# Half 1's causal convolution as four TensorE products in a fused state-space, expert and attention kernel

## The chip, the cores and the metric

The kernel runs on one core of one Trainium2 chip. The metric is the device time of one execution in microseconds; every time in this text is in microseconds unless marked otherwise. PE is TensorE, DVE is VectorE, ACT is ScalarE, POOL is GpSimd and SP is SyncE.

## The reference, cut to what matters

Four stages follow each other, each added to `x` of shape (4, 256, 256): a selective state-space layer gated by the layer norm of `x`, a routed network with 32 experts (8 per token), cross attention with 16 heads, and a network with 16 experts (2 per token) and a shared one. Only the first stage is touched:

```python
x = einsum('ed,bld->bel', in_proj_w, ctx)            # 256 channels
xc = causal depthwise convolution of x, 4 taps        # per channel
u = silu(xc + conv_b)
x_dbl = einsum('ke,bel->bkl', x_proj_w, u)            # 8 rows dt, 16 B, 16 C
delta = softplus(dt_proj_w @ x_dbl[:8] + dt_proj_b)
# per channel and state n: state = state*exp(delta*A[n]) + delta*u*B[n];  y += state*C[n]
y = (y + D*u) * silu(layernorm(x))
```

## The kernel before, in words

**Tiling.** The 1024 tokens are two halves of 512 (two batches of 256 each). Channels stand on the 128 partitions, in two blocks (c = 0, 1), so one array of a half is 128x512 per block. The scan over time is one VectorE instruction (`tensor_tensor_scan`, L1544) per half and state over both blocks, 128x1024; there are 16 states (`DS`), and thus 16 steps per half. A step `n` consists of: ScalarE's decay exp(delta*A) (`scan_decay`, L1085, into one of two pairs of PSUM banks for half 0), the row of B spread over the partitions by a DMA (`b_rows`), GpSimd's product of it with delta*u (`scan_drive`, L2183; VectorE makes the first itself, L1534), the scan (L1544), the read-out with the row of C (`scan_read`, L1554) and TensorE's turning sum of the read-outs (`y_sum`, L571). Decay n+2 waits for scan n, drive n+1 for read-out n-1, and row n+3 of B for the drive that frees its buffer.

**Ahead of the first scan.** For each half and block TensorE makes `in_proj @ ctx` (`project_in`, L534), ScalarE the last tap (`first_tap`, L1053), VectorE three further taps in place, each over both batches (`convolve`, L1470), ScalarE the silu (`activate_u`, L1058). Then x_dbl (`project_x_dbl`, L542) is copied by ScalarE (`move_x_dbl`, L1049), dt is one product on a bias product (`bias_dt` L559, `project_dt` L551), ScalarE takes exp and ln (`activate_delta`, L1069 and L1071), VectorE bounds it (L1517) and multiplies with u (L1523). `x_dbl`'s rows go to DRAM by `store_bc` and come back as `b_rows` and `c_rows`. Both halves are prepared before or just within the first steps of the first scan; the normalisation of `x` for the gate (statistics L1479, L1484, L1486 on VectorE, the power -1/2 on GpSimd, `scale_norm`, L2141, shift L1510) lies in the same stretch.

**What sets the order.** Every engine has its own instruction stream, executed in the order written; semaphores join them. In the first scan ScalarE's stream holds, after the decay of step n+2, work for the gate (`normalise_z`, `activate_z`), TensorE's the folding of the attention weights (`fold_turn`, `fold_multiply`, at the steps listed in `folds_at`: from step 4, two at steps 7, 10 and 13), and SyncE's the loads: at every step one row of B, one row of C, and, at their steps, weights of the first expert layer (`fetch(0)` to `fetch(3)`, 384 KB each), raw attention weights (`load_fold`, 384 + 256 KB) and folded ones (`store_fold`, 512 KB). A row of B or C is 256 KB. ScalarE swaps its function table (`preload_act_table_set`) between silu, log/exp and exp.

After the first scan VectorE gates y, adds it to `x` and makes the next statistics; the turned `x` gives the router its logits, and the second half's scan runs between the first expert products. From about 200 us on TensorE works nearly without a gap to the end.

## Time and profile before

| | us |
|---|---|
| median of 3 runs (lowest to highest) | 672.03 (671.31 to 673.62) |
| span of the profiled execution | 671.5 |
| PE busy in it (share of the span) | 619.0 (92%) |
| DVE busy | 485.6 (72%) |
| ACT busy | 412.6 (61%) |
| POOL busy | 305.0 (45%) |

The profile shows one execution by its span, from the first to the last instruction; the page gives no other time of its own for it. An engine's busy share is a mean over stages with different limits. So the profile is to be read by stage: which engine has no idle time there, and what ended the wait of the one that had.

### The profile page before, as it was taken

Reading aid. Unit: us, or ns where it says so; the run is one execution under the profiler, and the core shown is the slowest. Engines: PE = TensorE matmul, PEld = TensorE weight load, DVE = VectorE, ACT = ScalarE, POOL = GpSimd, SP = SyncE. Lnnn points to the kernel's source line nnn. Section 1 sums busy time; section 2 is a strip of 40 time slices with the busy share of each in tenths; the row PEclk is TensorE's granted clock in tenths of the full one; section 3 lists DMA queues with packets and bytes.
Section 4 is the critical chain, followed back from the end, with each engine's and each line's share of the span. In section 5 each row is a group of like instructions: output and inputs, shape, how many; then the busy total and the mean of one; then the engine's idle time right before and its main releaser. Section 6 shows DMA issues by size and latency. Waiting matters only on the chain.

```text
span 671.5 us, 11179 instructions
## 1 busy us (share of the span) xinstructions
PE 619.0 (92%) x3740; PEld 517.2 (77%) x3740; DVE 485.6 (72%) x1048; ACT 412.6 (61%) x846; POOL 305.0 (45%) x304
## 2 busy tenths in 40 slices
PE   6768669999999999999999999999999998899994
PEld 2356445566777788888888999999989988789983
DVE  5999889999987665546457766767759774785464
ACT  4976565855535645445457787777867768654441
POOL 1456630022254434445436656665545788540214
PEclk9668988999999999999999999999999999999998
DMA  6686744666764364454319533224101112255654
GB/s 199 189 291 226 280 162 132 198 202 205 211 171 137 97 175 136 136 156 155 125 48 313 189 120 117 79 79 138 53 32 33 56 64 87 80 173 156 197 160 132
DMA packets 58135, 98.90 MB, mean 147 GB/s; under 512 B 7000, under 2 KB 26976, under 8 KB 58080
## 3 DMA queue, kind: packets, MB, share of 16 engines
q1 hardware_dynamic: 56544, 94.00, 44.1%
q0 software_dynamic: 1536, 4.20, 1.9%
q8 instruction: 31, 0.51, 0.3%
q14 instruction: 24, 0.20, 0.1%
HBM read 78.51 MB, written 19.66 MB: 146 GB/s over the span
## 4 chain that ended last, share of the span: by engine, by line
PE 65%; DVE 19%; issue 5%; ACT 4%; POOL 3%; DMA 2%; DVEq 0%; POOLq 0%; SPq 0%; ACTq 0%
PE bank L101 18%; PE bank L102 17%; PE bank L103 17%; DVE state L1544 7%; PE bank L886 3%; PE bank L974 3%; DVE read_out L1554 3%; PE bank L938 2%; PE bank L571 1%; DVE u_sb L1470 1%; PE bank L680 1%; DMA b_rows<-bc_scratch 1%; ACT probs L1341 1%; DVE stats L1479 1%; DVE head_out_lo L1461 1%
## 5 line engine op out<-in xcount | busy, mean ns | idle before, releaser
L2149 POOL TENSOR_TENSOR w_lo<-w_raw,w_hi 128x512 fp32r<-128x512 f32 (+1 forms) x78 | 120.6, 1549 | 160.5 <-ACT w_hi L1049 80.0
L101 PE MATMUL bank<-xt_hi,w_hi 128*128 128x512 f32 x256 | 104.7, 409 | 1.6 <-POOL w_lo L2149 1.0
L103 PE MATMUL bank<-xt_hi,w_lo 128*128 128x512 f32 x256 | 101.1, 395 | 0.0
L102 PE MATMUL bank<-xt_lo,w_hi 128*128 128x512 f32 x256 | 100.9, 394 | 0.0
L1049 ACT ACTIVATE w_hi<-w_raw 128x512 fp32r<-128x512 f32 (+1 forms) x78 | 56.6, 726 | 45.9 <-PE bank L103 45.0
L1341 ACT ACTIVATE probs<-scores,row_min 128x256 f32<-128x256 f32 x128 | 63.8, 501 | 17.4 <-DVE row_min L1963 17.4
L2260 POOL TENSOR_TENSOR probs<-probs,row_scale 128x512 f32<-128x512 f32 x64 | 66.6, 1040 | 5.0
L1963 DVE CUSTOM_DVE_ANT_0 scores<-bank,mask_bias 128x256 f32<-128x256 f32 x128 | 48.8, 420 | 17.3 <-PE bank L103 17.3
L571 PEld LDWEIGHTS bank<-identity,read_out 128*128 128x128 f32 x272 | 36.3, 159 | 30.4 <-DVE read_out L1554 18.6
L1049 ACT ACTIVATE probs_t_hi<-bank 128x512 fp32r<-128x512 f32 x64 | 38.2, 597 | 32.6 <-PE bank L886 32.3
L101 PEld LDWEIGHTS bank<-xt_hi,w_hi 128*128 128x128 f32 x256 | 48.2, 188 | 12.4 <-POOL w_lo L2149 3.6
L103 PEld LDWEIGHTS bank<-xt_hi,w_lo 128*128 128x128 f32 x256 | 48.1, 188 | 11.7
L571 PE MATMUL bank<-identity,read_out 128*128 128x128 f32 x272 | 41.6, 306 | 15.8 <-DVE read_out L1554 13.2
L102 PEld LDWEIGHTS bank<-xt_lo,w_hi 128*128 128x128 f32 x256 | 48.3, 189 | 8.5 <-issue 0.2
L1461 DVE TENSOR_TENSOR probs_t_lo<-bank,probs_t_hi 128x512 fp32r<-128x512 f32 x64 | 44.1, 689 | 10.4 <-ACT probs_t_hi L1049 10.2
L2183 POOL TENSOR_TENSOR drive<-delta_u,b_rows 128x1024 f32<-128x1024 f32 x16 | 38.4, 2401 | 28.4 <-DVE read_out L1554 17.5
L2257 POOL TENSOR_TENSOR row_scale<-row_scale,any_valid 128x2 f32<-128x2 f32 x64 | 12.5, 195 | 76.3 <-DVE row_scale L1955 76.1
L1461 DVE TENSOR_TENSOR hidden_lo<-bank,hidden_hi 128x512 fp32r<-128x512 f32 x34 | 23.4, 690 | 31.4 <-ACT hidden_hi L1049 31.4
L101 PE MATMUL bank<-probs_t_hi,ctx_tok_hi 128*128 128x256 f32 x128 | 41.4, 323 | 4.7 <-DVE head_out_lo L1461 4.6
L1554 DVE TENSOR_TENSOR read_out<-state,c_rows 128x1024 f32<-128x1024 f32 x32 | 42.5, 1330 | 0.6
L1842 DVE TENSOR_TENSOR bank<-gated,bank 128x512 f32<-128x512 f32 x34 | 23.6, 695 | 26.0 <-PE bank L103 22.6
L1207 ACT ACTIVATE gated<-bank 128x512 f32<-128x512 f32 x48 | 28.7, 597 | 22.2 <-PE bank L103 22.1
(259 smaller groups left out, 1834.2 us busy)
## 6 DMA issues: line engine op xcount, KB each, us to landing
w_raw<-in_ffn_w SPq DMA_DIRECT2D x46, 384.0 KB, 3.5
b_rows<-bc_scratch SPq DMA_DIRECT2D x32, 256.0 KB, 4.9
c_rows<-bc_scratch SPq DMA_DIRECT2D x32, 256.0 KB, 4.3
w_raw<-fold_scratch SPq DMA_DIRECT2D x32, 256.0 KB, 2.7
experts<-in_ffn_w SPq DMA_DIRECT2D x16, 384.0 KB, 4.3
route_bc<-route_scratch SPq DMA_DIRECT2D x31, 192.0 KB, 3.4
...
```

Source lines behind the costliest of these rows:

```text
L101: e.matmul(out, w_hi, m_hi, start=first, stop=False)
L102: e.matmul(out, w_hi, m_lo, start=False, stop=False)
L103: return e.matmul(out, w_lo, m_hi, start=False, stop=last)
L571: last = e.matmul(ps[:, l * DI + c * P:l * DI + (c + 1) * P], tile[:, c, t:t + P], identity[:, :], is_transpose=True, start=n < 0 and l + ...
L1049: e.activation(out, source, ACT.Copy).then_inc(sem(name), 1)
L1341: last = e.activation(probs[i % 3][:, r, :], scores_sb[i % 2][:, r, :], ACT.Exp, scale=-1.0, bias=row_min[i % 2][:, r:r + 1], accum_out=ro ...
L1461: e.tensor_tensor(out_lo, source, out_hi.bitcast(F32), ALU.subtract).then_inc(sem(name), 1)
L1544: e.tensor_tensor_scan(flat2(state[i % 2][:, :, :]), flat2(factor[:, :, :]), flat2(drive[i % 2][:, :, :]), 0.0, ALU.mult, ALU.add).then_in ...
L1554: e.tensor_tensor(read_out[n % 4][:, :, :], state[i % 2][:, :, :], c_rows[i % 3][:, :].unsqueeze(1).broadcast_to([P, EH, HT]), ALU.mult).t ...
L1963: e.tensor_tensor_reduce(scores_sb[i % 2][:, r, :], bank[4 + i % 2][:, r * SEQ:(r + 1) * SEQ], mask_bias[:, half * HB + b, :], -SCALE, 3.0 ...
L2149: e.tensor_tensor(lo[:, 0:n], w_raw[(p - WHOLE) % RAW][:, 0:n], hi[:, 0:n].bitcast(F32), ALU.subtract).then_inc(sem("w_lo"), 1)
L2260: e.tensor_tensor(probs[i % 3][:, :, :], probs[i % 3][:, :, :], row_scale[i % 3][:, :].unsqueeze(2).broadcast_to([P, 2, SEQ]), ALU.mult).t ...
```

## The change

- Half 0 goes first on all engines. `ctx`'s half 0 is loaded from ScalarE's queue, the small weights come second and the projections third on SyncE, half 1's `ctx` and the raw attention weights later.
- Half 0's block 0 is projected, tapped and convolved batch by batch; the order of waits between the six small taps leaves one other tap between two that depend on each other. VectorE instead of ScalarE copies its x_dbl.
- Half 1 is no longer projected and convolved in two steps. TensorE turns the taps (`turn_conv`), VectorE copies them (`conv_rows`), TensorE spreads each tap's row over the partitions (`spread_conv`, with a selection matrix made on GpSimd), VectorE multiplies `in_proj` by it (`scale_in_proj`, one 128x1024 instruction) and TensorE sums four products of 512 columns per block, each with `ctx` shifted by one token more (`convolve`). The silu reads that bank.
- Half 1's u is made at step 0 of the first scan, its x_dbl is moved at step 1, its delta comes at steps 3 to 5 (before the read-outs of 4 and 5), `activate_z` at step 5 instead of 2.
- GpSimd makes delta*u of half 0's block 0. Half 1's variance and half 0's shift lie between scan 0 and read-out 0, half 1's shift after it.
- Folding starts at step 5, with two at 7, 9, 11 and 13; `fetch(0)` and `fetch(1)` move to steps 4 and 5, `fetch(2)` and `fetch(3)` behind the first scan.

The diff, cut to its core:

```diff
@@ -492,8 +498,10 @@
...
-        FOLD_FROM, FOLD_STEPS = 4, 2 * KV_HEADS
-        FOLD_TWICE = (7, 10, 13)
+        FOLD_FROM, FOLD_STEPS = 5, 2 * KV_HEADS
+        FOLD_TWICE = (7, 9, 11, 13)
+        LATE_U, LATE_DELTA, Z_AT = 0, 3, 5
...
@@ -504,8 +512,12 @@
...
         def dt_bank(h, c):
-            return ((7, 0), (6, 1))[h][c]
+            return ((7, 0), (7, 6))[h][c]
...
@@ -527,29 +539,57 @@
...
+            def turn_conv():
+
+                at.wait_ge("consts", 3)
+                at.wait_ge("ld_small", 16)
+                for c in range(EH):
+                    last = e.transpose(bank[4][0:DC, c * P:(c + 1) * P], small_sb[:, c, 0:DC], identity[:, :])
+                last.then_inc(sem("conv_in"), CONV_TURNED)
+
+            def spread_conv(taps):
+
+                at.wait_ge("conv_in", CONV_ROWS)
+                at.wait_ge("gpsimd_chain", 3)
+                for j in taps:
+                    e.matmul(bank[4 + j // 2][:, j % 2 * DI:(j % 2 + 1) * DI], conv_pick[:, j * P:(j + 1) * P],
+                             conv_rows[:, :], start=True, stop=True).then_inc(sem("conv_in"), 1)
+
+            def convolve(c):
+
+                at.wait_ge("conv_in", CONV_SCALED)
+                at.wait_ge("ld_ctx1", 16)
+                ps = take(6 + c, ("u", EH + c + 1))
+                out_of = ps.rearrange("p (b s) -> p b s", b=HB)
+                ctx_of = ctx_sb[:, HT:].rearrange("p (b s) -> p b s", b=HB)
+                for back in range(DC):
+                    last = e.matmul(out_of[:, :, back:], conv_in[:, DC - 1 - back, c * P:(c + 1) * P],
+                                    ctx_of[:, :, :SEQ - back], start=back == 0, stop=back == DC - 1)
+                last.then_inc(sem("conv_in"), 1)
...
+            def project_x_dbl(h, c):
...
-                ps = take(6, ("x_dbl_sb", h + 1))
-                for c in range(EH):
-                    at.wait_ge("u", 2 * h + c + 1)
-                    last = e.matmul(ps[0:DR + 2 * DS, :], x_proj_sb[:, c, :], u_sb[:, h, c, :],
-                                    start=c == 0, stop=c == EH - 1)
-                last.then_inc(sem("x_dbl"), 1)
-
-            def project_dt(h):
+                ps = take(6, ("x_dbl_sb", h + 1)) if c == 0 else bank[6]
+                at.wait_ge("u", 2 * h + c + 1)
+                last = e.matmul(ps[0:DR + 2 * DS, :], x_proj_sb[:, c, :], u_sb[:, h, c, :],
+                                start=c == 0, stop=c == EH - 1)
+                if c == EH - 1:
+                    last.then_inc(sem("x_dbl"), 1)
...
@@ -781,25 +821,33 @@
...
-            for c in range(EH):
-                project_in(0, c)
-            for c in range(EH):
-                project_in(1, c)
...
-            at.wait_ge("consts", 3)
+            turn_conv()
+            for b in range(HB):
+                project_in(0, b, slice(b * SEQ, (b + 1) * SEQ))
+            project_in(1, 0, slice(0, HT))
+            spread_conv(range(2))
+            project_x_dbl(0, 0)
+            spread_conv(range(2, DC))
+            bias_dt(0, 0)
+            project_x_dbl(0, 1)
+            bias_dt(0, 1)
             for c in range(EH):
-                bias_dt(0, c)
-            project_x_dbl(0)
-            project_dt(0)
-            project_x_dbl(1)
+                project_dt(0, c)
             for c in range(EH):
-                bias_dt(1, c)
-            project_dt(1)
+                convolve(c)
             for n in range(-1, DS):
                 y_sum(0, n)
-                if n == 1:
+                if n == LATE_U:
+                    for c in range(EH):
+                        project_x_dbl(1, c)
+                if n == LATE_DELTA - 1:
+                    for c in range(EH):
+                        bias_dt(1, c)
+                        project_dt(1, c)
+                if n == Z_AT - 1:
                     turn_z(0)
                     turn_z(1)
...
@@ -1048,15 +1096,19 @@
...
-            def first_tap(h, c):
-                at.wait_ge("proj_in", 2 * h + c + 1)
...
+            def first_tap(c, b, tokens, nth):
+                at.wait_ge("proj_in", nth)
+                e.activation(u_sb[:, 0, c, tokens], bank[in_bank(c, b)][:, tokens], ACT.Copy,
                              scale=conv_w[DC - 1][:, c:c + 1]).then_inc(sem("first_tap"), 1)
...
-                at.wait_ge("conv", 2 * h + c + 1)
-                e.activation(u_sb[:, h, c, :], u_sb[:, h, c, :], ACT.Silu,
-                             bias=conv_b[:, c:c + 1]).then_inc(sem("u"), 1)
+                if h == 0:
+                    at.wait_ge("conv", HB + c)
+                    source = u_sb[:, 0, c, :]
+                else:
+                    at.wait_ge("conv_in", CONV_SCALED + c + 1)
+                    source = bank[6 + c][:, :]
+                e.activation(u_sb[:, h, c, :], source, ACT.Silu, bias=conv_b[:, c:c + 1]).then_inc(sem("u"), 1)
...
@@ -1226,35 +1277,40 @@
...
+            e.dma_start(ctx_sb[:, 0:HT], ctx_t[:, 0:HT]).then_inc(sem("ld_ctx0"), 16)
             e.preload_act_table_set("silu_and_others")
...
-            first_tap(0, 0)
-            first_tap(0, 1)
-            first_tap(1, 0)
+            for b in range(HB):
+                first_tap(0, b, slice(b * SEQ, (b + 1) * SEQ), b + 1)
+            first_tap(1, 0, slice(0, HT), HB + 1)
             activate_u(0, 0)
-            first_tap(1, 1)
             activate_u(0, 1)
-            move_x_dbl(0)
-            activate_u(1, 0)
-            activate_u(1, 1)
             e.preload_act_table_set("natural_log_exp_and_others")
             e.activation(decay[:, :, :], a_log, ACT.Exp).then_inc(sem("a_exp"), 1)
             activate_delta(0)
-            move_x_dbl(1)
             for n in range(2):
                 scan_decay(0, n)
-            activate_delta(1)
             make_skip(0)
-            normalise_z(0)
             for n in range(DS):
                 if n + 2 < DS:
                     scan_decay(0, n + 2)
-                if n == 0:
+                if n == LATE_U:
+                    e.preload_act_table_set("silu_and_others")
+                    activate_u(1, 0)
+                    activate_u(1, 1)
+                    e.preload_act_table_set("natural_log_exp_and_others")
+                if n == LATE_U + 1:
+                    normalise_z(0)
+                    move_x_dbl(1)
+                if n == LATE_U + 2:
                     normalise_z(1)
-                if n == 2:
+                if n == LATE_DELTA:
+                    activate_delta(1)
+                if n == Z_AT:
+                    e.preload_act_table_set("silu_and_others")
                     activate_z()
                     e.preload_act_table_set("exp_and_others")
...
@@ -1460,20 +1516,43 @@
...
+            def convolve(c, back, batches):
...
+                late = u_sb[:, 0, c, :].rearrange("p (b s) -> p b s", b=HB)[:, batches, back:]
+                x_in = bank[in_bank(c, batches.start)][:, :].rearrange("p (b s) -> p b s", b=HB)[:, batches, :SEQ - back]
+                return e.scalar_tensor_tensor(out=late, in0=x_in, scalar=conv_w[DC - 1 - back][:, c:c + 1], in1=late,
+                                              op0=ALU.mult, op1=ALU.add)
...
+            def convolve_by_batch():
+
                 for back in range(1, DC):
...
+                    for b in range(HB):
+                        at.wait_ge("first_tap", b + 1)
+                        if back > 1:
+                            at.wait_ge("vector_chain", own.count - (HB - 1 if back < DC - 1 else HB - 1 - b))
+                        last = convolve(0, back, slice(b, b + 1))
+                        if back < DC - 1:
+                            own.step(last)
+                        else:
+                            last.then_inc(sem("conv"), 1)
+
+            def convolve_whole():
+
+                at.wait_ge("first_tap", HB + 1)
+                for back in range(1, DC):
+                    own.settle()
+                    last = convolve(1, back, slice(0, HB))
                     if back < DC - 1:
                         own.step(last)
-                        own.settle()
                 last.then_inc(sem("conv"), 1)
...
+            def scale_in_proj():
+
+                at.wait_ge("conv_in", CONV_SPREAD)
+                at.wait_ge("ld_in_proj", 16)
+                e.tensor_tensor(conv_in[:, :, :], banks[:, 4:6, :].rearrange("p k (j d) -> p (k j) d", j=2),
+                                in_proj_sb[:, :].unsqueeze(1).broadcast_to([P, DC, DI]),
+                                ALU.mult).then_inc(sem("conv_in"), 1)
...
@@ -1855,32 +1934,44 @@
...
-            for c in range(EH):
-                convolve(0, c)
-            for c in range(EH):
-                convolve(1, c)
+            at.wait_ge("conv_in", CONV_TURNED)
+            e.tensor_copy(conv_rows[:, :], bank[4][0:DC, 0:DI]).then_inc(sem("conv_in"), 1)
+            at.wait_ge("ld_small", 16)
+            convolve_by_batch()
+            convolve_whole()
             at.wait_ge("ld_x0", 16)
             for j in range(HC):
                 chunk_stats(0, j)
             find_variance(0)
-            at.wait_ge("conv", 2 * HALVES)
+            at.wait_ge("x_dbl", 1)
+            e.tensor_copy(x_dbl[:, 0:HT], bank[6][0:DR + 2 * DS, :]).then_inc(sem("x_dbl_sb"), 1)
+            scale_in_proj()
+            at.wait_ge("a_exp", 1)
+            e.tensor_scalar(decay[:, :, :], decay[:, :, :], -1.0, None, ALU.mult).then_inc(sem("decay_ready"), 1)
+            at.wait_ge("conv", HB + 1)
+            at.wait_ge("conv_in", CONV_SCALED)
             e.memset(banks[:, 2:6, :].rearrange("p k (b s) -> p (k b) s", b=HB)[:, :, 0:1],
                      0.0).then_inc(sem("decay_ready"), 1)
             at.wait_ge("ld_x1", 16)
-            for j in range(HC):
+            for j in range(2):
                 chunk_stats(1, j)
-            find_variance(1)
-            at.wait_ge("a_exp", 1)
-            e.tensor_scalar(decay[:, :, :], decay[:, :, :], -1.0, None, ALU.mult).then_inc(sem("decay_ready"), 1)
-            find_z_shift(0)
-            make_delta_u(0)
+            make_delta(0, 0)
+            chunk_stats(1, 2)
+            make_delta(0, 1)
+            make_delta_u(0, 1)
             scan_drive(0, 0)
-            find_z_shift(1)
+            chunk_stats(1, 3)
             for n in range(DS):
                 scan_state(0, n)
+                if n == 0:
+                    find_variance(1)
+                    find_z_shift(0)
+                if n in (LATE_DELTA + 1, LATE_DELTA + 2):
+                    make_delta(1, n - LATE_DELTA - 1)
+                    make_delta_u(1, n - LATE_DELTA - 1)
                 scan_read(0, n)
                 if n == 0:
-                    make_delta_u(1)
+                    find_z_shift(1)
...
@@ -2156,6 +2247,13 @@
...
+            own.step(e.memset(conv_pick[:, :], 1.0))
...
@@ -2189,8 +2287,13 @@
...
             split_gates()
             scale_norm(0, 1)
+            at.wait_ge("delta", 1)
+            at.wait_ge("u", 1)
+            e.tensor_tensor(delta_u[:, 0, 0, :], delta[:, 0, 0, :], u_sb[:, 0, 0, :],
+                            ALU.mult).then_inc(sem("delta_u"), 1)
+            scan_drive(0, 1)
             scale_norm(1, 2)
-            for n in range(1, DS):
+            for n in range(2, DS):
                 scan_drive(0, n)
             scan_drive(1, 0)
...
@@ -2373,38 +2476,39 @@
                 e.dma_start(out_dram[:, t:t + 2, :], x_tok[:, t:t + 2, :]).then_inc(sem("out_stored"), 16)
 
             load(in_proj_sb[:, :], in_proj_t, "ld_in_proj")
-            for h in range(HALVES):
-                load(ctx_sb[:, h * HT:(h + 1) * HT], ctx_t[:, h * HT:(h + 1) * HT], f"ld_ctx{h}")
             load(small_sb[:, :, :], ssm_small, "ld_small")
+            load(x_proj_sb[:, :, :], x_proj_t, "ld_proj")
+            load(dt_proj_sb[:, :], dt_proj_t, "ld_proj")
             for c in range(EH):
                 e.dma_start(dt_row[0:1, c * P:(c + 1) * P], ssm_small[:, c, DC + 2:DC + 3].rearrange("p a -> a p"),
                             allow_slow_non_contiguous=True).then_inc(sem("ld_proj"), 16)
             for h in range(HALVES):
                 load(x_tok[:, h * HC:(h + 1) * HC, :], x_dram[:, h * HC:(h + 1) * HC, :], f"ld_x{h}")
-            load(x_proj_sb[:, :, :], x_proj_t, "ld_proj")
-            load(dt_proj_sb[:, :], dt_proj_t, "ld_proj")
+                if h == 0:
+                    load(ctx_sb[:, HT:], ctx_t[:, HT:], "ld_ctx1")
             load(gate_raw[:, :, :], gate_t, "ld_late")
             load(cent_raw[:, :, :], centroids_t, "ld_late")
             load(bias_bc[:, :], rows(gate_bias, P), "ld_late")
             load(mask_u8[:, :, :].rearrange("p b s -> p (b s)"), rows(key_mask, P), "ld_late")
-            for g in range(2):
-                load_fold(g)
 
 
             store_bc(0)
             for n in range(3):
                 load_b(0, n)
                 load_c(0, n)
+                if n < 2:
+                    load_fold(n)
             load_b(0, 3)
-            store_bc(1)
             for n in range(DS):
                 if n > 0:
                     load_b(*divmod(n + 3, DS))
                 load_c(*divmod(n + 3, DS))
-                if n < SPLIT:
-                    fetch(n)
+                if n == LATE_U + 2:
+                    store_bc(1)
                 if n + 2 < FOLD_RAW:
                     load_fold(n + 2)
+                if 0 <= n - FOLD_RAW + 1 < 2:
+                    fetch(n - FOLD_RAW + 1)
                 for g in range(KV_HEADS):
                     if g >= FOLD_RAW and fold_step[2 * (g - FOLD_RAW) + 1] + 1 == n:
...
@@ -2413,6 +2517,8 @@
...
             load_c(1, 3)
+            for p in range(2, WHOLE):
+                fetch(p)
             store_fold(KV_HEADS - 2)
             load_b(1, 5)
             load_c(1, 4)
```

## Rows read from the trace of the kernel before

**Rows 1.** The page's chain that ended last, share of the span by engine and line

```profile
PE 65%; DVE 19%; issue 5%; ACT 4%; POOL 3%; DMA 2%; DVEq 0%; POOLq 0%; SPq 0%; ACTq 0%
```

**Rows 2.** Instructions in order of time, VectorE (start, duration, line, shapes, count, idle before)

```profile
7.38 8.96 DVE L1470 SCALAR_TENSOR_TENSOR u_sb<-bank,small_sb,u_sb 128x510 f32<-128x510 f32 x12 [7.38 <-ACT u_sb L1053]
...
24.22 2.29 DVE L1544 TENSOR_TENSOR_SCAN state<-bank,drive 128x1024 f32<-128x1024 f32 x1
...
27.69 1.28 DVE L1517 SCALAR_TENSOR_TENSOR delta<-delta,bank 128x512 f32<-128x512 f32 x2
28.88 2.58 DVE L1523 TENSOR_TENSOR delta_u<-delta,u_sb 128x512 f32<-128x512 f32 x2
...
87.86 1.37 DVE L1554 TENSOR_TENSOR read_out<-state,c_rows 128x1024 f32<-128x1024 f32 x1
```

**Rows 3.** Groups by line, VectorE, 24.2 to 89.2 us

```profile
L1544 DVE TENSOR_TENSOR_SCAN state<-bank,drive 128x1024 f32<-128x1024 f32 x16 | 36.5, 2279 | 2.3 <-POOL drive L2183 2.3
```

**Rows 4.** Order of time, SyncE's queue, before the first scan

```profile
2.17 0.43 SPq L2300 DMA_DIRECT2D small_sb<-in_ssm_small  x1
...
17.06 0.33 SPq L2300 DMA_DIRECT2D b_rows<-bc_scratch  x1
```

**Rows 5.** Order of time, TensorE, before the first scan

```profile
4.42 6.61 PE L534 MATMUL bank<-ctx_sb,in_proj_sb 128*128 128x512 f32 x8 [4.42 <-DMA ctx_sb<-in_ctx_t]
...
12.87 1.91 PE L542 MATMUL bank<-u_sb,x_proj_sb 128*40 128x512 f32 x4
15.46 2.13 PE L551 MATMUL bank<-x_dbl,dt_proj_sb 8*128 8x512 f32 x4 [0.68 <-ACT x_dbl L1049]
17.52 3.41 PE L542 MATMUL bank<-u_sb,x_proj_sb 128*40 128x512 f32 x4
```

**Rows 6.** Order of time, ScalarE, before the first scan and at its third step

```profile
11.94 0.72 ACT L1058 ACTIVATE u_sb<-u_sb,small_sb 128x512 f32<-128x512 f32 x1 [0.15 <-DVE u_sb L1470]
...
17.12 1.28 ACT L1243 ACT_TABLE_LOAD   x1
...
18.55 0.58 ACT L1069 ACTIVATE delta<-bank 128x512 f32<-128x512 f32 x1
...
37.15 1.30 ACT L1085 ACTIVATE bank<-delta,decay 128x510 f32<-128x510 f32 x2 [1.80 <-DVE state L1544]
```

**Rows 7.** One line's instructions, ns min/median/max; last row b_rows' landing in us

```profile
L1554 DVE TENSOR_TENSOR read_out<-state,c_rows x16: 1225/1371/2636, 26.5 to 87.9; 128x1024 f32<-128x1024 f32 x16
...
L1523 DVE TENSOR_TENSOR delta_u<-delta,u_sb x4: 679/685/1973, 21.6 to 30.8; 128x512 f32<-128x512 f32 x4
...
DMA to landing us min/median/max: 3.2/5.6/7.8
```

**Rows 8.** Order of time, GpSimd, at three places

```profile
18.35 1.05 POOL L2141 TENSOR_TENSOR rstd<-rstd,half_power 128x4 f32<-128x4 f32 x1 [5.03 <-DVE rstd L1486]
...
24.25 2.34 POOL L2183 TENSOR_TENSOR drive<-delta_u,b_rows 128x1024 f32<-128x1024 f32 x1 [2.96 <-DVE drive L1534]
...
95.92 2.92 POOL L2141 TENSOR_TENSOR rstd<-rstd,half_power 128x4 f32<-128x4 f32 x1 [7.77 <-DVE rstd L1486]
```

**Rows 9.** Windows: busy time of each engine, granted clock, DMA share, GB/s

```profile
15.00:20.00 5.00, 4.54 (x7) 1.25 (x8) 4.86 (x20) 4.58 (x8) 1.05 (x1) 0.72 0.38 81
...
25.00:30.00 5.00, 2.43 (x7) 0.94 (x6) 4.97 (x5) 4.49 (x9) 3.66 (x2) 0.50 0.49 98
```

**Rows 10.** Who waited for whom, 14 to 90 us: total, times, longest

```profile
POOL drive L2183 <- DMA b_rows<-bc_scratch: 7.9, 3, 3.7
```

**Rows 11.** Chain that ended last, 60 to 80 us (start, us, what)

```profile
67.94 7.22 DMA b_rows<-bc_scratch
...
75.28 3.10 POOL drive L2183
...
78.46 2.30 DVE state L1544
```

**Rows 12.** DMA of the stretch 16 to 50 us, all queues

```profile
DMA packets 3954, 8.11 MB, mean 238 GB/s; under 512 B 458, under 2 KB 458, under 8 KB 3951
```

65 lines of the change are left out of this document (33 added, 32 removed).

## The prediction, made before the changed kernel ran

> **What bounds the kernel now.** I read the page first: the chain that ended last is 65% TensorE and 19% VectorE [rows 1]. TensorE's share is nearly all the 128x512 split products that come after the state-space layer; the change touches none of them. So the change can only help by letting that part begin earlier, and the question is how much earlier the first scan (half 0, 16 states) ends. The trace in order of time answers what sets that: VectorE is busy, with one gap of 2.3, from its first convolution tap at 7.38 us to the last read-out of the first scan, which ends at 87.86 + 1.37 = 89.23 us [rows 2]. Within the scan (24.22 to 89.23) it does 16 scans of 2.28 [rows 3] and 16 read-outs of 1.23 to 1.37; one pair takes 3.5 to 3.6. Behind the scan stands one unbroken chain (gate, add, statistics, turn, router, second scan, then TensorE), so I count each microsecond at 89.23 as one microsecond at the end. The profiled span is 671.5; it lies 0.5 under the median of the runs, 672.03, and I carry that 0.5 over. A difference under 0.3% (2.0 us) can't be told from no change.
>
> **Half 0 until its first scan.** ctx half 0 is now issued by ScalarE's queue, about when SyncE issues in_proj, and the small weights go second on SyncE instead of fourth (2.17 us [rows 4]); three issues of about 0.45 sit before it now, one afterwards, so it lands about 0.9 sooner. TensorE's first product began at 4.42 and eight instructions took 6.61 [rows 5], 1.7 per 512 columns at first. Now two small transposes of the taps come first (0.5, my estimate from these products' speed), then the two batches of channel block 0 as 256-column products, 0.85 each. First outputs at about 5.7, 6.5 and, for block 1, 8.2 us.
> Convolution on VectorE: 12 instructions took 8.96 [rows 2], 0.75 each. Kept for half 0 are 6 halves (0.75 less 256 elements at the 512 elements' rate, 0.48) and 3 whole ones: 2.9 + 2.3 = 5.2, but with gaps for the late first taps. Laid end to end behind first taps of 0.7 the last ends at 11.8, and the second silu near 12.5, against 11.94 + 0.72 = 12.66 before [rows 6]. **Splitting by batch alone gains almost nothing.**
> TensorE now has two tap spreads and a bias product between the two x_dbl products; they delay the second by about 0.5, so x_dbl is there at 14.0, against 12.87 + 1.91 = 14.78 [rows 5]. VectorE copies it now (not in the trace as such; between ScalarE's 0.58 for a 512-column read of a bank [rows 6] and a tap's 0.75, I take 0.65), dt of block 0 is there at 15.9, against 15.46 and half of 2.13 before [rows 5].
> The real gain is on ScalarE: before, its exp of dt began at 18.55, because half 1's taps and silus and the table load at 17.12 stood ahead [rows 6], two microseconds after dt was there. Now the table is loaded at about 13.8, exp begins at 16.0, and four activations of 0.6 end at 18.4, against 20.9. VectorE has free time for the scaling of in_proj (1024 elements a row, as one read-out of 1.23 [rows 7]: it ends at 15.9), the decay sign, and most of half 1's statistics. Then: second delta 19.15, delta_u 19.9 (block 0's goes to GpSimd, about half of a drive's 2.34 [rows 8], beside it), first drive 21.2, last statistic, first scan at 21.6. The b_rows load: its store issues at 14.8, it at 16.5 instead of 17.06 [rows 4], and 3.2 later (the fastest landing [rows 7]) it is in at 19.7, in time. **Start of the scan: 24.22 - 21.6 = 2.6 gained.** Bounds: 0.7 if only x_dbl's own lead (14.78 - 14.0) gets through; 4.5 if all of the six removed convolution instructions (6 x 0.75) do. I keep 2.6.
>
> **Half 1 inside the scan.** The eight tap products (4 taps x 2 blocks, each one 512-column fp32 product) follow dt from 16.9. Between 15 and 20 the granted clock was 0.72, from 25 to 30 it was 0.50, the lower of the two levels (1.2 GHz) [rows 9]; the same four x_dbl instructions took 1.91 and then 3.41 [rows 5]. So a product costs 0.86 at full clock and 1.7 at half: the eight take 6.9 to 13.7 and end at 23.8 to 30.6. I take 25.6 (half clock until about 20.8, then full, since these are full-array products back to back). ScalarE wants them at 26.5: decay of state 2 after the first scan, then a table load (1.28). Its extra work per step is 3.96 (two loads, two silus), 2.7, 2.1, 2.4 and 5.0 (z), against 2.2 free a step (3.52 less 1.30 for the decay [rows 6]) and 3.45 of one-time lead; the backlog peaks near 2.9, so it is hidden at no cost. If the lead were used up each further microsecond would be on the path.
> Delta of half 1: the four VectorE instructions cost 1.28 + 2.58 before [rows 2], where one delta_u ran beside a drive on GpSimd and took 1.97 instead of 0.69 [rows 7]. Moved between scan and read-out, when GpSimd is done, they cost 2.7, and I add 0.6 for the first log being late (bias and dt now come after step 2's turns at half clock): 0.3 to 0.5 gained at most. I take 0.3.
> **A new knot at step 0.** half 1's variance and half 0's shift are now between scan 0 and read-out 0: 0.7. And shift 1 after read-out 0 waits for GpSimd's power, which is behind drive 1 on GpSimd. A power took 1.05 alone but 2.92 beside a VectorE scan with both inputs in SBUF [rows 8]; a read-out ran 2.64 instead of 1.37 beside a late drive [rows 7]. I reckon drive 1 at 23.0 to 25.35 (its row is queued behind c_rows 0 and a fold load), the read-out held until 25.35 and ending 26.5, the power ending 27.4, shift, scan 1 at 27.6. Without any of this scan 1 would begin at 25.2. Cost 2.4; ends 0.7 (only the moved instructions) and 3.5 (another 1.1, a read-out, lost).
> The Trainium skill, SBUF — State Buffer, "Who interferes with whom", says that a VectorE instruction with two SBUF inputs and a GpSimd one that reads SBUF take turns, the first holding the port for its whole length. This trace agrees (2.64, 2.92). By a mere sharing of bandwidth the knot would be 0.7 and the time 1.7 less, 666.9.
>
> **Loads.** Three drives waited for b_rows, 7.9 in all [rows 10]; the first two, at steps 5 and 6, stretched two read-outs by 0.45 and (to 2.64 [rows 7]) 1.4. Steps 0 to 3 carried a whole weight piece (384 KB) each beside three folds (640 KB). Now those steps hold only folds, and two of the pieces come at steps 4 and 5, two after the scan. So the 1.85 is gained; ends 0 and 1.85. The later stall: b_rows for state 13 took 7.22 from issue to landing behind a fold store and fold load, its drive began at 75.28, scan 13 at 78.46 [rows 11], VectorE idle for 2.3 [rows 3]. The new plan spreads the doubled folds over 7, 9, 11, 13: from row 10 to row 12, 2816 KB must land in 10.9 us, before 4992 KB in 18.0; both about 0.27 MB/us, near the rate that failed. So a stall stays, a step earlier. I take 1.3 of it, so 1.0 gained; ends -2.3 and +2.3. The two whole pieces issued after the scan are first used some 15 us later, and landings took 5 to 8: covered. If that cover were gone, gate 2 would be late by the difference.
>
> **Sum.** -2.6 (start) -0.3 (delta) +2.4 (knot) -1.85 (early rows) -1.0 (late row) = **-3.35**. Span 671.5 - 3.35 = 668.1; with the 0.5, 668.6.
>
> **Rivals.**
> (a) *More.* The knot shrinks to 0.7 (row 1 lands in time and the power slips in during the scan) and no row is late: -2.6 -0.3 +0.7 -1.85 -2.3 = -6.4: 665.7, and up to 664 with the start at its better end. For: the early DMA load is lighter by 1.3 MB. Against: the power's 2.92 [rows 8] and the 7.22 of one row [rows 11]. Chance 0.17.
> (b) *The change does not do what it says / is given back.* Half 1's products stay at half clock to 30.6; x_dbl and dt of half 1 then take 3.4 each, the first log comes 1.4 later, and the start gains only 0.7 because x_dbl of half 0 is what sets it: -3.35 + 1.4 + 1.9 = -0.05, 672.0; with either alone -1.5 to -1.95, so 670.1 to 670.5. For: clock 0.50 in this stretch before [rows 9]. Against: TensorE now works where it was idle. Chance 0.17. The Trainium skill, TensorE: Matmul & The Clock Gate, "What's actually happening", says that the default is the throttled state and that activity releases it; by that rule these products release it themselves, and the forecast stands; this trace has both levels, but no stretch of such products here.
> (c) *Slower.* Late b_rows decide: the first rows are now interleaved with two fold loads (issued around 18 us, before they went at 8 us under the convolutions), and folds follow in steps 0, 1, 2. If the queue gives less than one fold and two rows (1152 KB) in 3.6 us, which is 0.32 MB/us, each of drives 1 to 6 is late, and a late one costs up to 2.3 idle plus 1.3 for the blocked read-out. From 16 to 50 us the mean was 238 GB/s [rows 12]. One such drive (3.6) beyond what I took evens the gain out; two at 2.7 each make it 668.6 + 5.4 = 674.0. For: loads of b_rows took 5.6 us to land at the median [rows 7]. Against: these rows are each issued over 4 us before use. Chance 0.09.
> The forecast itself keeps 0.57.
>
> **Numbers.** Predicted 668.6. The forecast's own ends are 667 and 670; the range reaches to (a)'s and (b)'s cases: 664.8 to 671.4. Faster by over 0.3% (under 670.0): 0.52 of the forecast, (a) whole, a little of (b): 0.72. Within 0.3%: 0.20. Slower: 0.08.
>
> **What would show it.** The first scan of half 0 starts near 21.6, the second near 27.6 after a gap, the last read-out ends near 85.8; the eight tap products lie between 16.9 and 25.6; ScalarE loads a table four times in the scan's first 30 us; no VectorE idle before the scans of steps 3 to 9. Wrong would be: scans waiting for the decay on ScalarE (the lead was used up), a first scan still after 23, or several scans that wait for a GpSimd drive.

## The result, and the profile after

The changed kernel takes **679.12** (median of 4 runs, 677.90 to 680.78) against 672.03: ratio **1.0105** [1.009, 1.0121], slower by 7.1. Forecast were 668.6 and a range from 664.8 to 671.4. It was run again on two other chips: 1.0113 [1.009, 1.0135] (678.95 against 671.67) and 1.0111 [1.0092, 1.013] (687.58 against 679.12). So 1.011 is the yardstick for all that follows. Ratios to the kernel before on the same chip are compared, since on three of the five chips that were used the kernel before itself takes 7 to 8.5 longer. A ratio is estimated from all runs and can differ by up to 0.002 from the quotient of the two medians given beside it (here 687.58/679.12 is 1.0125); no smaller difference between two ratios is relied on.

The page's chain of the profiled execution (span 676.2, its time 678.25) is that of before [rows 1] but for a larger share of TensorE and a smaller one of VectorE:

```profile
PE 67%; DVE 16%; issue 5%; ACT 4%; POOL 3%; DMA 3%; SPq 0%; DVEq 0%; POOLq 0%; ACTq 0%
```

VectorE in order of time (start, duration, engine, line and operation, idle before it and what ended it), which answers to [rows 2]:

```profile
15.94 0.68 DVE L1947 COPY x_dbl<-bank 40x512 f32<-40x512 f32 x1 [2.24 <-PE bank L582]
...
20.93 0.69 DVE L1595 SCALAR_TENSOR_TENSOR delta<-delta,bank 128x512 f32<-128x512 f32 x1 [2.29 <-ACT delta L1123]
...
22.64 0.69 DVE L1595 SCALAR_TENSOR_TENSOR delta<-delta,bank 128x512 f32<-128x512 f32 x1 [0.68 <-ACT delta L1123]
...
25.57 2.27 DVE L1623 TENSOR_TENSOR_SCAN state<-bank,drive 128x1024 f32<-128x1024 f32 x1
27.76 0.36 DVE L1563 BATCH_NORM_AGGREGATE mean_var<-stats 128x2 f32<-128x6 f32 x4
28.15 0.83 DVE L1565 TENSOR_SCALAR rstd<-mean_var 128x4 f32<-128x4 f32 x1
28.90 0.15 DVE L1589 SCALAR_TENSOR_TENSOR z_shift<-mean_var,rstd 128x4 f32<-128x4 f32 x1
28.97 1.21 DVE L1633 TENSOR_TENSOR read_out<-state,c_rows 128x1024 f32<-128x1024 f32 x1
31.09 2.31 DVE L1589 SCALAR_TENSOR_TENSOR z_shift<-mean_var,rstd 128x4 f32<-128x4 f32 x1 [0.91 <-POOL rstd L2232]
33.33 2.28 DVE L1623 TENSOR_TENSOR_SCAN state<-bank,drive 128x1024 f32<-128x1024 f32 x1
...
47.53 0.69 DVE L1595 SCALAR_TENSOR_TENSOR delta<-delta,bank 128x512 f32<-128x512 f32 x1 [1.25 <-ACT delta L1123]
...
91.56 1.37 DVE L1633 TENSOR_TENSOR read_out<-state,c_rows 128x1024 f32<-128x1024 f32 x1
...
95.67 1.30 DVE L1642 TENSOR_TENSOR bank<-bank,z_gate 128x512 f32<-128x512 f32 x2 [1.61 <-PE bank L611]
...
103.37 1.38 DVE L1575 TENSOR_SCALAR x_norm<-x_tok,mean_var,rstd 128x256 f32<-128x256 f32 x4 [0.83 <-POOL rstd L2232]
```

Three things stand in it. Before, VectorE had no wait from its first tap to the first scan; now it waits 5.2 in three places for half 0's own x_dbl and dt. The two four-element instructions at 28.15 and 31.09, 0.17 and 0.15 when alone, take 0.83 and 2.31. And the gate waits 1.61 for TensorE, twice the 0.8 of before. GpSimd shows what the small ones stood beside, a drive each time:

```profile
26.60 2.36 POOL L2281 TENSOR_TENSOR drive<-delta_u,b_rows 128x1024 f32<-128x1024 f32 x1 [3.63 <-DMA b_rows<-bc_scratch]
29.06 1.99 POOL L2232 TENSOR_TENSOR rstd<-rstd,half_power 128x4 f32<-128x4 f32 x1
31.03 2.35 POOL L2281 TENSOR_TENSOR drive<-delta_u,b_rows 128x1024 f32<-128x1024 f32 x1
```

TensorE ahead of the scan, to be read against [rows 5], and the stretches of [rows 9] (columns: length, then busy time and instructions of PE, PEld, which is TensorE's weight load, DVE, ACT and POOL, then the granted clock, 1.00 being the 2.4 GHz level, DMA share, GB/s):

```profile
10.45 1.02 PE L582 MATMUL bank<-u_sb,x_proj_sb 128*40 128x512 f32 x2 [0.45 <-ACT u_sb L1111]
11.40 1.13 PE L563 MATMUL bank<-conv_rows,conv_pick 4*128 4x256 f32 x4
12.37 1.68 PE L599 MATMUL bank<-ones,dt_row 1*128 1x512 f32 x2
13.97 1.93 PE L582 MATMUL bank<-u_sb,x_proj_sb 128*40 128x512 f32 x2
15.83 2.07 PE L599 MATMUL bank<-ones,dt_row 1*128 1x512 f32 x2
17.70 3.62 PE L591 MATMUL bank<-x_dbl,dt_proj_sb 8*128 8x512 f32 x4
21.24 9.56 PE L574 MATMUL bank<-ctx_sb,conv_in 128*128 128x512 f32 x16
```
```profile
8.00:12.00 4.00, 3.55 (x10) 1.56 (x10) 3.93 (x8) 1.61 (x3) 0.69 (x3) 1.00 0.58 184
12.00:15.00 3.00, 3.00 (x7) 0.70 (x5) 1.63 (x9) 2.03 (x3) 1.32 (x3) 0.60 0.00 0
15.00:20.00 5.00, 5.00 (x7) 1.83 (x6) 2.66 (x6) 0.36 (x1) 0.00 (x0) 0.50 0.17 39
20.00:25.00 5.00, 5.00 (x7) 1.70 (x6) 3.31 (x5) 3.67 (x7) 1.27 (x1) 0.50 0.94 247
```

From 12 on the small products run at the lower level: an x_dbl product pair takes 1.93 instead of 1.02. The engine is never idle there, and all that stands on half 0's path is behind it. ScalarE had its function table by 13.82 and then waited:

```profile
19.64 0.60 ACT L1121 ACTIVATE delta<-bank 128x512 f32<-128x512 f32 x1 [5.58 <-PE bank L591]
```

**The balance of the two traces**, from [rows 2, 3] to these. The first scan starts at 25.57 instead of 24.22: +1.35. Step 0, from scan 0 to scan 1, takes 7.76, before 7.16: +0.60. Steps 4 and 5 take 10.63, before 8.91: +1.72. The late row costs the same (5.85, one state earlier, as forecast). From the last scan's start to the normalised x it takes 14.13, before 13.32: +0.81. Sum +4.48; the normalised x is at 103.37 instead of 98.87, and the rest is 572.8 long, 0.2 more. That gives the 4.7 between the spans. Of before it rests on these lines and [rows 2]:

```profile
31.38 2.28 DVE L1544 TENSOR_TENSOR_SCAN state<-bank,drive 128x1024 f32<-128x1024 f32 x1
...
42.04 2.28 DVE L1544 TENSOR_TENSOR_SCAN state<-bank,drive 128x1024 f32<-128x1024 f32 x1
...
50.95 2.28 DVE L1544 TENSOR_TENSOR_SCAN state<-bank,drive 128x1024 f32<-128x1024 f32 x1
...
98.87 1.38 DVE L1496 TENSOR_SCALAR x_norm<-x_tok,mean_var,rstd 128x256 f32<-128x256 f32 x4 [0.83 <-POOL rstd L2141]
```

The medians are 7.1 apart, which the two spans and three estimates make up: before's profile was one of its longer executions (671.5 and the 1.8 that every later run of that kernel has outside its span is 673.3, 1.3 over its median), after's was 0.9 under its own median, and after has 2.05 outside its span. A pair profiled on one chip is told below.

### The profile page after: what moved, and what is told of

It reads as the page before. It is cut to its first block, busy times and chain, and to the rows that moved or that the text cites. A ratio compares the mean times of both kernels' runs of the same rounds, so it can differ in the third digit from the quotient of the medians.

```text
span 676.2 us, 11234 instructions
## 1 busy us (share of the span) xinstructions
PE 630.8 (93%) x3764; PEld 521.0 (77%) x3764; DVE 482.9 (71%) x1047; ACT 413.8 (61%) x846; POOL 309.2 (46%) x308
## 4 chain that ended last, share of the span: by engine, by line
PE 67%; DVE 16%; issue 5%; ACT 4%; POOL 3%; DMA 3%; SPq 0%; DVEq 0%; POOLq 0%; ACTq 0%
PE bank L101 17%; PE bank L102 17%; PE bank L103 17%; DVE state L1623 5%; PE bank L934 3%; PE bank L1022 3%; DVE read_out L1633 3%; PE bank L611 2%; DMA b_rows<-bc_scratch 2%; PE bank L986 1%; PE bank L720 1%; ACT probs L1397 1%; POOL rstd L2232 1%; DVE head_out_lo L1517 1%; POOL back L2332 1%
## 5 line engine op out<-in xcount | busy, mean ns | idle before, releaser
L1517 DVE TENSOR_TENSOR probs_t_lo<-bank,probs_t_hi 128x512 fp32r<-128x512 f32 x64 | 44.1, 690 | 10.4 <-ACT probs_t_hi L1097 10.2
L2360 POOL TENSOR_TENSOR row_scale<-row_scale,any_valid 128x2 f32<-128x2 f32 x64 | 12.5, 195 | 76.3 <-DVE row_scale L2046 76.2
L1633 DVE TENSOR_TENSOR read_out<-state,c_rows 128x1024 f32<-128x1024 f32 x32 | 40.6, 1267 | 0.5
```

The lines of the kernel that those rows point to most:

```text
L1517: e.tensor_tensor(out_lo, source, out_hi.bitcast(F32), ALU.subtract).then_inc(sem(name), 1)
L1633: e.tensor_tensor(read_out[n % 4][:, :, :], state[i % 2][:, :, :], c_rows[i % 3][:, :].unsqueeze(1).broadcast_to([P, EH, HT]), ALU.mult).t ...
```

## Experiments

In what follows, "scan 0" is the start of the first scan, "to x" the time from there to the normalised x.

**One chip, both kernels as they are.** Before: span 670.6, scan 0 at 24.16, normalised x at 98.28, time 672.39. After: span 676.7, scan 0 at 25.90, normalised x at 103.56, time 678.74. Here every part can be placed: start +1.74, step 0 +0.26, steps 4 and 5 (10.64 against 9.50) +1.14, the late row and two more late ones +2.1, tail +0.06, rest of the kernel +0.8, outside the span +0.25. Together 6.35, which is the difference of the two times. Which rows are late changes from one execution to the next. A third profile of after, on the last chip, had scan 0 at 25.89, step 0 at 7.51 and 78.6 to x.

**Half 1's shift behind scan 1.**

```diff
-                if n == 0:
-                    find_z_shift(1)
+                if n == 1:
+                    find_z_shift(1)
```

> Theory K (knot at step 0): in the changed kernel scan 1 began at 33.33, 5.5 after scan 0 ended, because half 1's shift waited for GpSimd's power and then 2.3 for drive 2. Here that one shift moves behind scan 1. Theory K: scan 1 begins within 3.0 of scan 0's end instead of 5.5, and the kernel is 2 to 3 us faster than the changed one (679.1), near 676.5. Theory C (clock: the loss lies in TensorE running at half clock on half 0's path and in delta of half 1): scan 1 begins earlier but other waits (decays on ScalarE) take its place, under 1 us gained, near 678.5.

Ratio 1.0065 [1.0038, 1.0093], against 1.011 some 3 us less. VectorE in order of time, from scan 1 on:

```profile
30.09 2.28 DVE L1623 TENSOR_TENSOR_SCAN state<-bank,drive 128x1024 f32<-128x1024 f32 x1
32.29 1.10 DVE L1589 SCALAR_TENSOR_TENSOR z_shift<-mean_var,rstd 128x4 f32<-128x4 f32 x1
```

Step 0 falls from 7.76 to 4.37; step 1 grows by 0.9, since the shift now meets the last 1.1 of drive 2. To x: 74.1 instead of 77.8. One instruction of four elements, at another place, is worth some 40% of what the change lost (some 3 of 7.1; in the trace 3.7).

**Half 1's dt a step earlier.**

```diff
-                if n == LATE_DELTA - 1:
+                if n == LATE_DELTA - 2:
```

> Half 1's bias and dt products go on TensorE one step earlier (after step 1's turns instead of step 2's). Theory D (delta of half 1 is late only because TensorE starts it late at half clock): VectorE's wait of 1.25 before the first delta at step 4 goes, 1.0 to 1.5 us faster than the changed kernel, near 677.8. Rival: the wait moves to step 1 or 2 read-outs' turns or to the log, no gain, 679.

The step that held the wait fell from 5.98 to 4.63, by the whole wait of 1.25 and 0.1 more. The ratio was 1.0093 [1.0071, 1.0115], about 1 us less than 1.011 and inside the uncertainty. But scan 0 began at 27.85, though the code ahead of it is unchanged:

```profile
8.69 2.07 PE L563 MATMUL bank<-conv_rows,conv_pick 4*128 4x256 f32 x4
10.69 1.93 PE L582 MATMUL bank<-u_sb,x_proj_sb 128*40 128x512 f32 x2
12.54 2.07 PE L563 MATMUL bank<-conv_rows,conv_pick 4*128 4x256 f32 x4
14.41 1.91 PE L599 MATMUL bank<-ones,dt_row 1*128 1x512 f32 x2
```

In this execution every small product ran at the lower level from 8.69 on, some 3.5 sooner than in the profile of after, and the start came 2.3 later. The same text gives both: of nine profiles with TensorE's code ahead of the scan as in after, five have the lower level from about 12 on and scan 0 at 25.5 to 25.9, two have it from about 11 and scan 0 at 27.2 and 27.3, and two from 8.7 and scan 0 at 27.84 and 27.85. This is the most direct sign in the record that the level moves the start.

**The order of the small products.**

```diff
-            spread_conv(range(2, DC))
             bias_dt(0, 0)
             project_x_dbl(0, 1)
+            spread_conv(range(2, DC))
+            project_dt(0, 0)
             bias_dt(0, 1)
-            for c in range(EH):
-                project_dt(0, c)
+            project_dt(0, 1)
```

> On TensorE the bias of block 0 stands before the second tap spread, the second spread after the second x_dbl product, the bias of block 1 behind the first dt. Theory O (small products ahead of x_dbl and dt delay the path of half 0, more so at half clock): x_dbl ends about 1.3 earlier, dt of block 0 about 3, first scan begins near 23 instead of 25.57, 2 to 3 us faster, near 676.5. Theory C alone (only the level of the clock counts): under 1 us gained, since at half clock the same products follow.

Ratio 1.0098 [1.0079, 1.0117]; scan 0 at 26.80 where some 23 was expected, small products slow from about 11.5. No gain that can be told from none. Order alone does not help, as both tap spreads and both biases still stand ahead of half 0's second dt.

**Three full-array products between the small ones** (into banks not yet in use).

```diff
             spread_conv(range(2))
+            warm(5)
             project_x_dbl(0, 0)
+            warm(5)
             spread_conv(range(2, DC))
             bias_dt(0, 0)
             project_x_dbl(0, 1)
+            warm(1)
             bias_dt(0, 1)
```

> Three full-array products whose result nobody reads are added on TensorE: one before and one after the first x_dbl product, one while VectorE copies x_dbl. Theory C (the clock fell at about 12.6 because from 8.6 on TensorE held only small products): the clock stays at the upper level, x_dbl, bias and dt take 1.0, 1.0 and 1.9 instead of 1.9, 2.1 and 3.6, the first scan begins 2 to 3 us sooner in spite of the added work, near 676.5. Rival (the clock falls whatever is done here): the added 2.6 to 5.2 us of products are only partly hidden, the first scan begins 1 to 3 later, 680 to 682.

The products did run at the upper level (second x_dbl pair 1.05, dt 2.28 instead of 3.62), and scan 0 began at 24.21, 1.4 earlier than in the profile of after. One step later 0.5 of it was left:

```profile
24.21 2.27 DVE L1631 TENSOR_TENSOR_SCAN state<-bank,drive 128x1024 f32<-128x1024 f32 x1
...
26.79 1.75 DVE L1573 TENSOR_SCALAR rstd<-mean_var 128x4 f32<-128x4 f32 x1
...
30.65 2.30 DVE L1597 SCALAR_TENSOR_TENSOR z_shift<-mean_var,rstd 128x4 f32<-128x4 f32 x1 [0.91 <-POOL rstd L2240]
32.87 2.28 DVE L1631 TENSOR_TENSOR_SCAN state<-bank,drive 128x1024 f32<-128x1024 f32 x1
```

Drive 1 waits for its row of B and came at 26.16, only 0.4 earlier; so a scan 0 that ends earlier meets more of it. The ratio rose to 1.015 [1.0111, 1.0189], runs from 686.4 to 692.3. The profile doesn't explain that: its normalised x, at 103.01, is no later than after's.

**Half 1 convolved by VectorE ahead of the scan,** the rest of the change kept: no turned, spread and scaled taps, no tap products; two whole first taps and six convolution instructions more, and ScalarE copies x_dbl again.

```diff
-            turn_conv()
...
-            spread_conv(range(2))
+            for c in range(EH):
+                e.matmul(bank[4 + c][:, :], in_proj_sb[:, c * P:(c + 1) * P], ctx_sb[:, HT:],
+                         start=True, stop=True).then_inc(sem("proj_in"), 1)
             project_x_dbl(0, 0)
-            spread_conv(range(2, DC))
...
-            for c in range(EH):
-                convolve(c)
```

> The changed kernel with half 1 convolved by VectorE again, ahead of the scan (6 instructions of 0.75 behind half 0's), no tap turn, spread or scaling, ScalarE copies x_dbl; all else of the change stays. Theory T (TensorE's own part is what costs: spreads, and the products that come before half 1's u, fill half 0's path while VectorE stands idle for 6.6 before the scan): the first scan begins 1 to 3 sooner than in the changed kernel and the time is equal or up to 3 us less. Rival V (the TensorE convolution is worth its 4.5 of VectorE): 2 to 4.5 us slower than the changed kernel.

676.20 against 678.95 on that chip: ratio 1.0063 [1.0047, 1.008] against 1.0113, so TensorE's convolution, with the copy and the scaling that VectorE does for it, costs 2.8 net. Scan 0 began at 23.62, 2.3 earlier than in after on that chip, even with six more VectorE instructions ahead of it. Here too the addition before the power met drive 1 (2.33, its whole length) and step 0 took 9.23.

**The first two edits together.**

> Both repairs of the scan's first steps together: half 1's shift behind scan 1, half 1's dt one step earlier on TensorE. If they add: 2.7 + 0.8 less than the changed kernel, ratio to the kernel before 1.005. Rival (the backlog on ScalarE takes the place): no better than the first alone, 1.0065.

676.49, ratio 1.0079 [1.0063, 1.0096], and again on another chip 683.20, 1.0065 [1.0048, 1.0083]: 2.5 and 4.4 less than after's medians on these chips. Both steps fell as they did singly (4.35 and 4.63).

**The fold plan of before.**

```diff
-        FOLD_FROM, FOLD_STEPS = 5, 2 * KV_HEADS
-        FOLD_TWICE = (7, 9, 11, 13)
+        FOLD_FROM, FOLD_STEPS = 4, 2 * KV_HEADS
+        FOLD_TWICE = (7, 10, 13)
```

> Only the fold plan is put back: the first fold step at state 4 and the doubled ones at 7, 10, 13, instead of 5 and 7, 9, 11, 13. Theory A (the later fold plan is what makes the last y_sum late and so the normalised x 0.8 us later than the last read-out alone explains): the gap between the last read-out's end and x_norm falls from about 9.5 to 8.9 or less, and the time falls by 0.6 to 1.0 against the changed kernel. Rival B (the plan is not it; TensorE is late because the late convolution, x_dbl, dt and turned z of half 1 push the folds): nothing changes, and the scans start when they did, within 0.3. Rival C (the old plan with the new place of the loads makes more late rows): one or two more drives wait and the time rises by 1 to 4.

Ratio 1.0078 [1.006, 1.0096]. The gate, which waited 1.61, waits for nothing, and 8.9 lie between the last read-out and the normalised x (in after 10.4, not the 9.5 of the expectation). To x 76.96 instead of 77.8. The mended kernel below shows the same: with the plan of before the 11.0 from its last read-out to the normalised x became 8.9. So the later plan does make the last y_sum late. In the execution of after with two more late rows the gate stood at 95.86, in the one shown at 95.67: in both the last y_sum stood behind folds and began at 94.59 and 94.79, so that the folds set it and hid the rows.

**The first two fold loads ahead of the first rows**, where before had them.

```diff
+            for g in range(2):
+                load_fold(g)
             store_bc(0)
             for n in range(3):
                 load_b(0, n)
                 load_c(0, n)
-                if n < 2:
-                    load_fold(n)
```

> Only one thing is changed: the first two fold loads are issued before B and C of half 0 are stored, as the kernel before did, and not between the first rows. Theory A (the fold loads between the rows make row 1 of B land late, so the first drive on GpSimd runs into the end of scan 0 and holds the four-element instruction and the read-out): drive 1 starts before 25.3 instead of 26.6 and ends before scan 0 does, the reciprocal root's addition takes 0.2 instead of 0.8, the step from scan 0 to scan 1 falls from 7.7 to between 4.5 and 6.5, and the time by 1.2 to 3.0. Rival B (the wait is for the latency of the store and its load, not for the queue): drive 1 starts when it did, no difference, the time within 0.5. Rival C: the folds in front delay ctx or x loads before the scan: the first scan starts over 0.5 later.

Ratio 1.0086 [1.0066, 1.0105]. Drive 1 did not wait for its row:

```profile
27.72 2.36 POOL L2281 TENSOR_TENSOR drive<-delta_u,b_rows 128x1024 f32<-128x1024 f32 x1 [2.48 <-DVE drive L1613]
```

It began 0.1 before scan 0, in after 1.0 behind it, the addition took 0.17 and step 0 7.08. The run with the earlier dt, as slow ahead of the scan (scan 0 at 27.85), had drive 1 waiting for its row until 28.72; so the order of the loads makes the difference. Scan 0 was at 27.84 with all small products slow, so the predicted points in time do not compare, only the distances.

**All mended together:** VectorE's convolution, the loads first, the shift behind scan 1, dt a step earlier, each as in the diffs above; and a variant of it with variance and shifts ahead of scan 0:

```diff
             make_delta_u(0, 1)
-            scan_drive(0, 0)
             chunk_stats(1, 3)
+            find_variance(1)
+            find_z_shift(0)
+            scan_drive(0, 0)
+            find_z_shift(1)
...
-            scan_drive(0, 1)
             scale_norm(1, 2)
+            scan_drive(0, 1)
```

> Four edits together: half 1 convolved by VectorE ahead of the scan (as in the run without TensorE's convolution), the first two fold loads before the first rows, half 1's shift behind scan 1, and dt of half 1 a step earlier. What this keeps of the change: x_dbl of half 0 copied by VectorE, exp ahead of half 1's work on ScalarE, half 1's delta inside the scan, the load order later on. If the accounts so far add up (run without TensorE's convolution -2.8 against the changed kernel, the shift -2.7 and the earlier dt -1.3 within a step, the loads -1 to -2), the first scan starts near 23.6, scan 1 near 28.3, x_norm is at 96 to 97.5 and the time is 1 to 3 us below the kernel before, ratio 0.995 to 0.999. Rival: the gains are not additive because each exposes the same load of row 1 (drive 1 at 26.2 holds the read-out until 28.5): scan 1 at 29.7, time equal to before within 0.3%.

> As the run before it, but half 1's variance and both shifts stand ahead of the first scan (0.6 to 1.0 of work, part of it in the wait for the first row), and GpSimd raises the power before its first drive. Theory A (the loss in step 0 is the small instructions held by the drives): the first scan starts 0.5 to 1.0 later than in that run, but steps 0 and 1 take 3.6 to 4.6 each instead of 4.4 to 5.5, so that scan 2 starts 0.5 to 1.5 earlier, and the time is 0.5 to 1.5 lower than there. Rival B (row 1 of B sets scan 1 in both): scan 1 starts at the same time in both, and the times agree within 0.5.

The first: 678.97 against 680.20, ratio **0.9982** [0.9969, 0.9995]: 0.2% less than the kernel before, clear of the noise but under the 0.3% that the prediction took as the least to be told, and 1.3% less than after. Scan 0 at 22.64, scan 1 at 26.50, normalised x at 97.30:

```profile
11.00 1.05 PE L582 MATMUL bank<-u_sb,x_proj_sb 128*40 128x512 f32 x2
11.98 1.12 PE L599 MATMUL bank<-ones,dt_row 1*128 1x512 f32 x2
13.03 1.05 PE L582 MATMUL bank<-u_sb,x_proj_sb 128*40 128x512 f32 x2
14.02 1.12 PE L599 MATMUL bank<-ones,dt_row 1*128 1x512 f32 x2
14.98 2.38 PE L591 MATMUL bank<-x_dbl,dt_proj_sb 8*128 8x512 f32 x4
```
```profile
22.64 2.27 DVE L1624 TENSOR_TENSOR_SCAN state<-bank,drive 128x1024 f32<-128x1024 f32 x1
24.83 0.35 DVE L1564 BATCH_NORM_AGGREGATE mean_var<-stats 128x2 f32<-128x6 f32 x4
25.21 0.17 DVE L1566 TENSOR_SCALAR rstd<-mean_var 128x4 f32<-128x4 f32 x1
25.29 0.16 DVE L1590 SCALAR_TENSOR_TENSOR z_shift<-mean_var,rstd 128x4 f32<-128x4 f32 x1
25.36 1.22 DVE L1634 TENSOR_TENSOR read_out<-state,c_rows 128x1024 f32<-128x1024 f32 x1
26.50 2.28 DVE L1624 TENSOR_TENSOR_SCAN state<-bank,drive 128x1024 f32<-128x1024 f32 x1
```

The second x_dbl ends at 14.1 instead of 15.9. The variant gave 1.0017 [1.0003, 1.0031]; its shift, now after drive 0, met drive 1 once more, so that scan 0 was at 26.28 and scan 2 at 33.35, 2.5 later than in the run before it; neither of its two theories had this:

```profile
24.06 2.30 DVE L1590 SCALAR_TENSOR_TENSOR z_shift<-mean_var,rstd 128x4 f32<-128x4 f32 x1 [0.90 <-POOL rstd L2236]
```

**The dummies again, on top of shift and dt.**

> The run before it with three full-array 512-column products added between TensorE's small products ahead of the first scan (their results go to banks not yet in use). Theory A (the half clock on half 0's small products costs 2 to 3 us of the start): with the early meeting of the small instruction and drive 1 out of the way, the first scan starts at 24.0 to 24.6 in place of 25.6 to 27.2, step 0 does not grow as it did with the dummies alone (under 5 instead of 8.7), and the median falls by 1.5 to 3.0 against the run before it. Rival B (the dummies only move the wait: they cost as much as they give, and the row of state 1 or the drive of GpSimd sets scan 1): the first scan earlier, the second at the same time, the median within 0.7. Rival C (it was the cause of the wider spread of 686 to 692): again a spread over 4 us and a median higher by 1 to 2.

684.17 against 683.20 without them, ratios 1.0062 [1.0044, 1.008] and 1.0065: no gain, nearest to rival B, though the scan did not begin earlier. In the profile the first spread and the first dummy ran slow all the same (2.07 and 2.08 at 8.5 and 10.5), the upper level came after 12.5, and the dummies' own 1.1 to 2.1 each ate what it gave; scan 0 was at 26.49, without the dummies at 25.48.

**The mended kernel with before's fold plan.**

> The mended kernel (half 1 convolved by VectorE, fold loads 0 and 1 first, shift behind scan 1, dt a step earlier) with the fold plan of the kernel before as well. Theory A (the later fold plan costs 0.8 at the last y_sum, and makes the late row of state 12): first scan to normalised x falls from 74.7 to 73.9 or less, the ratio to the kernel before from 0.998 to 0.996 or 0.997. Rival B (the late row only moves to another state and takes as long): no difference, 0.998.

To x fell from 74.66 to 73.05, as theory A had it; the ratio did not: 0.9981 [0.9968, 0.9994], rival B by the time. The two kernels ran on different chips, so only their ratios compare.

## Why the prediction was wrong

By its own sum (-3.35), against the two profiles shown (+4.5 at the normalised x):

- **Start, -2.6 forecast, +1.35 measured: the largest miss, 3.95.** The step that failed is "two tap spreads and a bias product ... delay the second by about 0.5, so x_dbl is there at 14.0", and dt at 15.9. They were costed at full clock and too low even for it (in the mended kernel a bias alone takes 1.1), with the second bias ahead of dt left out. Measured, the second silu ended at 12.52, as forecast, but the second x_dbl ended at 15.9 and the first dt product at about 19.5. The spread, bias, x_dbl, bias and half of dt from 11.40 to 19.5 take 8.1; in the mended kernel bias, x_dbl, bias and half of dt (11.98 to 16.2) take 4.2. The 3.9 between them is, by subtraction, the spread (1.1) and the lower level (2.8), an estimate across two kernels. What the prediction said of ScalarE was right but had nothing to stand on: its engine was free from 14.1 on, and exp waited 5.58 for dt. VectorE's scaling of `in_proj` (1.21) lay in such a wait and cost nothing. The clock was considered for half 1's products only, where it cost nothing: they ended at 30.8, at the upper bound, and ScalarE wanted the first block's at 30.5 and did not wait.
  How far is the clock shown as the cause? That the products are slow and that x_dbl and dt end late by as much is in the rows; in the nine profiles above an earlier fall of the level goes with a start that is 1.3 to 2.4 later; taking TensorE's share of half 1 out of the front gained 2.8 net on the same chip. Buying the upper level with dummies gained nothing at the median. So what is shown is that small products ahead of half 0's dt are expensive; not that the clock alone could be mended.
- **The knot at step 0, 6.0 forecast for the step (27.6 less 21.6), 7.76 measured: 1.76.** Mechanism right, one wait too few. The prediction held the read-out back by drive 1 and let the shift pass freely. It had the power end 5.8 after scan 0 began, measured 5.5; all that is missing stands behind it. Measured, row 1 of B landed late and drive 1 ran over the end of scan 0, where it held the addition for 0.83; the power took 1.99; and the shift was held by drive 2 for 2.31. The Trainium skill, SBUF — State Buffer, "Who interferes with whom", has the rule: a VectorE instruction with two SBUF inputs contends with a GpSimd one that reads SBUF, and the shared ports are an exclusive lock. The trace agrees, for a four-element instruction as for a read-out. The prediction had cited it for the large instructions and did not apply it to the small one that it had itself put behind a power and ahead of a drive. The runs show the price: 3.4 of step 0, of which 0.9 comes back at step 1.
- **Half 1's delta and the early late rows, +1.4 forecast for steps 4 and 5 together, +1.72 measured.** The size and the reason are right: no drive is late there, each of the four instructions takes 0.69 or less, against 1.97 before [rows 7]. The log was late by 1.25 where 0.6 was taken; an earlier dt removes it.
- **The late row, -1.0 forecast, 0.0 measured.** The stall stayed at 2.3 and came at state 12, the step earlier that was named, but 1.3 was taken for it without a row. It is the chain of waits around 70 us that shows it, as in [rows 11]:

```profile
70.19 4.90 DMA b_rows<-bc_scratch
...
75.22 3.26 POOL drive L2281
```

- **Not in the sum: +0.8 at the last y_sum,** from the later fold plan. The prediction asked which loads the plan moves and not when TensorE ends it. In the same way the 0.8 that the rest of the kernel was longer on one chip, and 0.25 outside the span, had no term; neither was explained. The 0.25 (2.05 instead of 1.8) is not there without TensorE's convolution: 32 of 40 such runs have 1.8 outside the span, though the other eight have 2.3.
- The own time of the profile: "it lies 0.5 under the median" compared a span with a time. It did no harm, since the sum was a difference. Nor does the range reach to (b)'s case, as it says: (b) adds up to 672.0, the range ends at 671.4.

Of the rivals, (b) named the right cause, half clock, at the wrong products, and bounded it at no change. (c), the slower one, expected late rows of B at drives 1 to 6; only drive 1's was late, and it cost through what it blocked. (a) needed a small knot, a step 0 of some 4.3. It came only with the shift moved: 4.35 to 4.39, and 3.86 in the mended kernel.

What remains open: why, in one and the same text, the lower level begins at 8.7 or about 11 in some executions and at 12 in others; what made the kernel with the dummies alone longer at the median; and why the mended kernel's 1.6 shorter front with the old fold plan did not shorten the time.
